# The scatters of a tile sent out as a pair in the last attention group of a decoder layer with eight experts

## The reference, cut to what matters

```python
logits = flat_x @ W_router + b_router
top_vals, top_idx = jax.lax.top_k(logits, 2)
router_weights = softmax(logits where chosen, else -inf)
for e in range(8):
    h = relu(flat_x @ W1[e] + b1[e])
    y = h @ W2[e] + b2[e]
    final_output += y * router_weights[:, e]
```

## Time and profile before

| what | us |
|---|---|
| median of three runs | 1500.87 |
| lowest and highest of them | 1497.72, 1504.2 |
| the profiled execution's own time | 1497.46 |
| its span, first to last instruction | 1495.7 |
| TensorE busy | 1451.5 (97%) |
| VectorE busy | 1150.8 (77%) |
| ScalarE busy | 1028.0 (69%) |
| POOL busy | 621.8 (42%) |

### The profile page before, as it was taken

How to read it: one execution, slowest core, us unless ns; L and a number is a source line. 1 busy time by engine, 2 the same in 40 slices (tenths; PEclk the granted TensorE clock), 3 DMA queues, 4 the chain that set the end, 5 groups by cost and what they waited for, 6 DMA issues and landing times.

```text
span 1495.7 us, 28982 instructions
## 1 busy us (share of the span) xinstructions
PE 1451.5 (97%) x9248; PEld 855.4 (57%) x9248; DVE 1150.8 (77%) x2534; ACT 1028.0 (69%) x1896; POOL 621.8 (42%) x906
## 2 busy tenths in 40 slices
PE   8999999999999999999999999999999999999997
PEld 4523332243443334445333344337999999999997
DVE  7988888888788878888878887745788987665572
ACT  3276667767666776865766765797677888776683
POOL 5024332233342263442325332343446765454453
PEclk8999999999999999999999999999999999999999
DMA  5734153023050440305224030053668988999884
GB/s 140 150 52 79 30 127 44 16 29 44 29 128 30 71 80 22 44 2 128 54 50 84 16 43 30 29 188 98 175 187 238 272 241 239 250 263 259 258 249 105
DMA packets 82063, 170.98 MB, mean 114 GB/s; under 512 B 14676, under 2 KB 48584, under 8 KB 79224
## 3 DMA queue, kind: packets, MB, share of 16 engines
q1 hardware_dynamic: 66439, 143.49, 38.0%
q0 software_dynamic: 15424, 25.63, 8.3%
q10 hardware_dynamic: 48, 0.01, 0.0%
HBM read 131.19 MB, written 34.36 MB: 111 GB/s over the span
## 4 chain that ended last, share of the span: by engine, by line
PE 81%; DVE 6%; issue 3%; ACT 3%; DMA 3%; POOL 1%; SPq 1%; another core or an unknown queue 0%; POOLq 0%; ACTq 0%; DVEq 0%
PE ps L1378 15%; PE ps L1405 15%; PE ps L1362 13%; PE ps L1612 3%; PE ps L1614 3%; PE ps L1613 3%; PE ps L1633 3%; PE ps L1634 3%; PE ps L1635 3%; PE ps L1477 2%; PE ps L1511 2%; DVE sums L1847 2%; PE ps L1616 2%; ACT prob L1652 2%; PE ps L1640 1%
## 5 line engine op out<-in xcount | busy, mean ns | idle before, releaser
L1652 ACT ACTIVATE prob<-ps 128x512 f32<-128x512 f32 x1024 | 564.0, 605 | 271.0 <-PE ps L1362 260.5
L2228 POOL TENSOR_TENSOR prob<-prob,reach 128x128 f32<-128x128 f32 x448 | 204.1, 458 | 529.9 <-ACT prob L1652 525.7
L1405 PE MATMUL ps<-stacked_k,stacked_q 120*128 120x512 bf16 x1024 | 389.1, 385 | 9.9 <-DVE rmax L1849 4.0
L1847 DVE CUSTOM_DVE_ANT_0 sums<-ps,ramps 128x512 bf16<-128x512 f32 x480 | 328.9, 685 | 81.2 <-PE ps L1405 75.3
L1849 DVE TENSOR_REDUCE rmax<-ps 128x1 f32<-128x512 f32 x480 | 326.7, 687 | 66.2 <-PE ps L1405 63.4
L1362 PE MATMUL ps<-stacked_q,stacked_k 123*128 123x512 bf16 x1024 | 356.2, 381 | 7.5 <-ACT prob L1652 5.6
L1405 PEld LDWEIGHTS ps<-stacked_k,stacked_q 120*128 120x128 bf16 x1024 | 99.0, 98 | 324.1 <-DVE rmax L1847 121.8
L1378 PE MATMUL ps<-prob,values 128*32 128x512 f32 x2048 | 273.6, 606 | 3.0 <-POOL prob L2228 2.0
L2293 POOL DMA_INDIRECT out<-yo,token_of x71 | 141.3, 1990 | 180.9 <-DVE yo L2170 141.4
L1797 ACT ACTIVATE hid<-ps,w_now 128x256 f32<-128x256 f32 (+1 forms) x312 | 124.7, 452 | 91.4 <-PE ps L1614 60.9
L1362 PEld LDWEIGHTS ps<-stacked_q,stacked_k 123*128 123x128 bf16 x1024 | 99.2, 98 | 124.1 <-ACT prob L1652 72.1
(11 more groups left out here) (246 smaller groups left out, 2275.2 us busy)
## 6 DMA issues: line engine op xcount, KB each, us to landing
w_now<-in_w SPq DMA_DIRECT2D x78, 514.0 KB
w_now<-in_w SPq DMA_DIRECT2D x78, 512.0 KB
stacked_q<-parts_of_rows SPq DMA_DIRECT2D x84, 128.0 KB, 6.5
stacked_k<-parts_of_rows SPq DMA_DIRECT2D x84, 128.0 KB, 7.1
xi<-expert_rows SPq DMA_DIRECT2D x71, 130.0 KB
parts_of_rows<-q_part SPq DMA_DIRECT2D x21, 256.0 KB, 2.8
parts_of_rows<-k_part SPq DMA_DIRECT2D x21, 256.0 KB, 2.9
b_now<-in_b SPq DMA_DIRECT2D x39, 128.0 KB
```

The costliest lines, as they stand in the source:

```text
L1405: m = e.matmul(ps[:, bank, :], qa[i][0:MAX_ROW, hh, qt * P:(qt + 1) * P], ka[i][0:MAX_ROW, hh, kc * BANK:(kc + 1) * BANK], start=True, sto ...
L1652: e.activation(prob[:, u % NPROB, :], ps[:, score_bank(u), :], ACT.Exp, scale=SLOPE ** (k[0] % NG * HG + k[3])).then_inc(sem["exp"], 1)
L1847: e.tensor_tensor_reduce(sums_16[:, :], of, ramp_beside(qt % 4), 1.0, -3.0e38, ALU.add, ALU.max, into).then_inc(sem["maxed"], 1)
L2228: e.tensor_tensor(tile, tile, reach[:, hh, :], ALU.mult).then_inc(sem["ranged"], 1)
```

## The change

The plan's price of a scatter on POOL goes from 1.3 to 1.0 us, for all batches. Batch 2's scatters come from a new generator, `last_scatters`, which puts both scatters of a tile into the list together, once the plan's time is 0.1 us past the planned end of the pair before; both get the same count of exponentials to wait for. `scatters` now serves batches 0 and 1 alone, under the same two conditions as before. And the list `scattering` is advanced after each unit also while a side step is half done, for all three batches.

```diff
-    "pool": {..., "scatter": 1.3, ...},
+    "pool": {..., "scatter": 1.0, ...},
...
         if whole:
-            scattering.append(scatters(b))
+            scattering.append(scatters(b) if b < NB - 2 else last_scatters(b))
             if b == NB - 2:
                 yield from table(0)
...
         for tt in range(NT):
             for which in range(TOPK):
 
-                while b < NB - 2 and not now["calm"] or p.pe < p.made.get("scatter", 0.0) + (0.3 if b < NB - 2 else 0.1):
+                while not now["calm"] or p.pe < p.made.get("scatter", 0.0) + 0.3:
                     yield
                 add("scatter", b, tt, which)
                 p.after["scatter", b, tt, which] = p.counts["exp"]
                 yield
+
+    def last_scatters(b):
+        for tt in range(NT):
+            while p.pe < p.made.get("scatter", 0.0) + 0.1:
+                yield
+            for which in range(TOPK):
+                add("scatter", b, tt, which)
+                p.after["scatter", b, tt, which] = p.counts["exp"]
+            yield
...
             step_on(placing)
             step_on(staging)
-            step_on(scattering)
+            if scattering and next(scattering[0], "end") == "end":
+                scattering.pop(0)
```

More of the change, by code:

```diff
@@ L93 @@
             "w_low": 0.75, "scale_q": 0.4, "normed": 0.26},
-    "pool": {"ranged": 0.45, "rstd": 1.75, "mid": 0.63, "low": 1.2, "bias1": 0.7, "bias2": 0.7, "scatter": 1.3, "added": 1.6, "fetch": 0.9, "yo_weight": 1.5, "direct": 0.0},
+    "pool": {"ranged": 0.45, "rstd": 1.75, "mid": 0.63, "low": 1.2, "bias1": 0.7, "bias2": 0.7, "scatter": 1.0, "added": 1.6, "fetch": 0.9, "yo_weight": 1.5, "direct": 0.0},
 }
```

## The result

The changed kernel takes **1503.96 us** (median of 20 runs, 1500.28 to 1507.82); the kernel before took 1498.47 in 20 runs beside them. The ratio is 1.0036, with a 95% interval of 1.0027 to 1.0045: 5.5 us slower, where I had forecast 4.4 us faster. It is under the 0.5% that I called measurable, but with 20 runs each the interval leaves the sign in no doubt. The profiled execution took 1504.05 us (span 1502.2), so it is a fair sample.

The account below looks back on a forecast made before the run. TensorE, busy for 97% of the span, was taken as the bound, with recoverable idle and slow-clock time at the handover. Gap 3.0 plus clock 1.4 made 4.4 us: 1500.87 to 1496.5 us, range 1488 to 1504.5.

Parts of the forecast that it names:

- the handover: Between attention and expert blocks, 42 us: TensorE idles 3.66 us and restarts slowly; the place the change reaches.
- The gap: Handover: TensorE's 2.53 us wait for `xi` goes, so the first expert product starts 3.0 us earlier.
- The clock: First expert products after the handover: 1.4 us more if TensorE's clock holds at full, 0 if it falls.
- POOL's cadence and the landing: Batch 2's scatters 1.35 us apart, last starting at 1004.1; landed between 1006.5 and 1012.4, early enough to cost nothing.
- the price and the open rule: Batches 0 and 1: price 1.0 and scatters beside half-done side steps move scatters closer, later steps earlier; costed at nothing.
- the slow rival: Groups before the last: POOL falls behind and TensorE waits for its multiplies; 9.6 us lost, 1510.5 us; chance 0.06.
- (1): Batch 2's scatters in pairs, limited by POOL alone: last one starts at 1004.1 instead of 1015.90, 11.8 us earlier.
- step (3): Handover: last attention product still ends at 1019.82, first expert product starts at 1021.9 instead of 1024.91, 3.0 us gained.
- The last exponential ends several us away from 1018.7: Sign of a wrong forecast: the rearranged plan of batches 0 to 2, costed at nothing, moved more than the handover.

Follow-up runs that it names:

- e4: Changed kernel without the pairs: new price and scatters beside half-done side steps stay, batch 2's scatters go one at a time; 1493.05 us, 0.9971 of the kernel before.
- e2: Changed kernel with batch 2's scatter pairs let go one pair every six exponentials; 1493.34 us, 0.9976 of the kernel before.
- e3: Changed kernel with batch 2's scatters as singles, one every three exponentials; 1494.48 us, 0.9977 of the kernel before.
- e5: Changed kernel with batch 2's scatters as singles, the first ten four exponentials apart, the last six packed; 1493.57 us, 0.9978 of the kernel before.
- f1: Changed kernel with batch 2's 16 scatters all at once and the scatters' semaphore moved to a far number; 1492.94 us, 0.9969 of the kernel before, chip 2.
- s1: Changed kernel with batch 2's 16 scatters all at once and one unused semaphore shifting semaphore numbers by one; 1507.12 us, 1.0049 of the kernel before, chip 5.

## Why the prediction was wrong

**Read right: the handover.** The place, the releaser and the size were as the forecast had them. The gap: first expert product 2.1 us after the last attention product, measured 2.06 in the changed kernel and 2.06 in e4. The clock: 1.00 there, and from the first expert product to the second one's begin it took 1034.89 - 1032.99 = 1.90 us instead of 3.38, so the gain of the clock is 1.5 us (the 1.4 of the forecast, from the same two terms, is rounded down). SP's first `xi` load is issued at 1015.43, 15.5 us ahead of the end of the last attention product; 7 to 13 were forecast. Together some 4.5 us; e4, where the trouble is as small as before, measures 1498.15 - 1493.05 = 5.1, e2 4.8, e3 3.7, and e5, which keeps a wait of 0.98 us for `xi`, 3.8.

**Roughly right: POOL's cadence and the landing.** I took 1.35 us per scatter from four rows that hold a first, slow one; in a long row it is 1.27. The last scatter should have started 20.25 us after the first; it took 23.45, of which 4.1 are the two gaps where POOL waits for a late ScalarE (3.45 and 3.20 us from start to start, less 1.27 each). In f1, without them, it is 19.4. From the start of the last scatter, 1008.85, to SP's first `xi` load are 6.6 us, where 2.44 were the better bound; it cost nothing, as forecast. The bias operations start 6.4 us later (1009.85 for 1003.49), not at most 2, and cost nothing either: VectorE's sum that needs them waits for a matmul and starts at 1021.91.

**Right in the number, not in the account: the price and the open rule.** I costed them at nothing, but held that the scatters of batches 0 and 1 would move closer and the steps behind them earlier by a few us. They did not: the 16 of batch 1 start from 784.8 to 837.4 us, over 52.6 us as before, and before the last group one of them has changed places with a bias operation. e4 has both parts and nothing else, and its gain of 5.1 us, with the interval of its ratio 2 to 6, is no more than the handover explains. The waits of the attention product for POOL's multiply, which the slow rival needed, came twice and for 2.0 us as in the earlier trace rows; that rival did not happen.

**The step that failed** is (1): "I therefore reckon POOL as the limit". The density of the scatters was priced by what POOL and the DMA engines can do and by what waits for them, and TensorE, which waits for no scatter, was left at its old pace: step (3) keeps the end of the last attention product at 1019.82, and it came at 1030.93. The term that I put at nothing is, on the chips with waits, 8.7 to 10.0 us of ScalarE's waits for the changed kernel, 14 to 15 with all at once, about 1 for the first four scatters of the kernel before. Against before, with its 1.09, that is 7.6 to 8.9 more; with the gain of 4.4 it makes +3.2 to +4.5, and the slow clock of 996 to 1002 and 1010 to 1013 us stands beside it, not priced by a run of its own; measured +5.5. On the other kind it is 0. The 1.09 us wait of ScalarE at 988.94 was in the trace of before, straight behind the first four scatters, the only four in a row, and named a matmul as its releaser. The earlier trace rows begin at 1001 us. That row could have warned me, though the five late scatters of e4, which cost nothing, show that it is no price per scatter.

**The sign in the forecast.** "The last exponential ends several us away from 1018.7" was given as what would make it wrong, and it did; the reason given for it, a rearranged plan, was not the cause: in the two traces the instructions of TensorE, ScalarE and VectorE stand in the same order from first to last. A sign that catches the failure with the wrong reason beside it was luck.

## What to carry to other kernels

An engine that neither issues nor awaits a burst of transfers can still be slowed while it runs, through the time at which its increments are seen: look for consumers that wait behind a producer whose instruction ended long before, and look in the old trace for a place where a short burst already has such a wait. It warns, but it does not give the price. Space GpSimd's transfers as far apart as the deadline allows and not as closely as the queue can take them; one scatter every three exponentials gave 3.7 us here and a pair every six 4.8, on a chip where all at once loses 9.2. And when two sets of runs disagree, ask first which chip each ran on, and compare kernels only with others from the same chip.

## What the hardware showed that I had not expected

- The same program took 1490.24 us on one chip and 1506.86 on another, while the kernel before took 1497.94 and 1497.33 there: not a slower chip, but one on which one pattern is slow.
- On such a chip the increments of TensorE came 1.2 to 4.0 us behind its matmuls while scatters started 1.3 us apart, whereas TensorE followed ScalarE's exponentials by 0.05 us.
- The longest single wait that came of it was 7.9 us (s1), and the half clock, once begun in the changed kernel, stayed for six us (996 to 1002).
